# A decoder kernel on one core: first loads in order of use, scores over 32 partitions, conversions behind copies

## The reference

```python
x = LN(x + causal_attention_L0(x))       # 16 heads; q, k of 3 numbers, plus (q.dir)(k.dir); values of 16
x = LN(x + cross_attention_L0(x, ctx))   # 16 heads of 16, scores clipped, nan -> uniform
x = LN(x + sign_ffn_L0(x))               # weights +-1 from booleans: 512(256) -> 1024 -> 1024 -> 256
x = LN(x + grouped_attention_L1(x))      # 16 heads of 64, 4 groups
x = LN(x + cross_attention_L1(x, ctx))   # 8 heads of 64
x = LN(x + experts_L1(x))                # shared expert and top 2 of 8
```

## Time and profile before

| | before |
|---|---|
| runs, us | 1266.02, 1274.17, 1264.87; median 1266.02 |
| the profiled execution | 1272.5 us, its span 1270.6 us |
| PE busy | 1150.3 us, 91% |
| DVE, ACT, POOL busy | 719.7, 565.0, 105.4 us |
| mean granted PE clock | 0.956 |
| chain that ended last | PE 79%, DVE 9%, issue 5%, ACT 4%, DMA 1% |

### The profile page before, as it was taken

One profiled execution on the slowest core, in us unless ns is written; L12 is line 12 of the kernel. 1 busy time (PEld: TensorE's weight loads), 2 busy tenths in 40 slices (PEclk: granted clock), 3 DMA queues, 4 the chain that ended last, 5 costly groups with the idle time before them and its releaser, 6 DMA issues.

```text
span 1270.6 us, 19991 instructions
## 1 busy us (share of the span) xinstructions
PE 1150.3 (91%) x7418; PEld 720.2 (57%) x7418; DVE 719.7 (57%) x1054; ACT 565.0 (44%) x1084; POOL 105.4 (8%) x147
## 2 busy tenths in 40 slices
PE   4999999898988988869988999999999999998797
PEld 2453443442222322247866777877787887786465
DVE  4344445667888789661426466465646666673213
ACT  1344344154545555751214566456635564562210
POOL 0112232112100000010001000010001000100100
PEclk7799899898979999979999999999999999999799
DMA  7012212320000000000023233123634964400000
GB/s 205 14 51 100 89 37 100 115 76 1 1 1 1 1 1 1 1 18 1 1 67 112 62 91 74 34 52 83 150 85 100 214 144 101 101 18 1 1 17 17
DMA packets 56962, 74.20 MB, mean 58 GB/s; under 512 B 12443, under 2 KB 33446, under 8 KB 56870
## 3 DMA queue, kind: packets, MB, share of 16 engines
q1 hardware_dynamic: 53110, 69.26, 21.4%
q10 hardware_dynamic: 3760, 3.67, 0.9%
HBM read 36.20 MB, written 15.73 MB: 41 GB/s over the span
## 4 chain that ended last, share of the span: by engine, by line
PE 79%; DVE 9%; issue 5%; ACT 4%; DMA 1%; POOL 1%; SPq 1%; ACTq 0%; POOLq 0%; DVEq 0%
PE p_unit L1665 20%; PE p_ring L1665 12%; PE p_out L1789 9%; PE p_ring L1685 8%; PE p_ring L1766 8%; PE p_ring L1732 7%; PE p_out L1755 6%; DVE halves L1454 2%; PE p_unit L1857 2%; PE p_ring L1710 1%; ACT prob_b L1238 1%; DVE prob_a L1468 1%; DVE x L1560 1%; PE p_ring L1724 1%; PE p_ring L1703 1%
## 5 line engine op out<-in xcount | busy, mean ns | idle before, releaser
L1454 DVE TENSOR_REDUCE halves<-p_ring 128x2 f32<-128x1024 f32 x128 | 156.2, 1220 | 65.8 <-PE p_ring L1710 65.6
L1252 ACT ACTIVATE prob_a<-p_ring 128x1024 f32<-128x1024 f32 x128 | 130.6, 1022 | 101.6 <-PE p_ring L1732 101.4
L1434 DVE TENSOR_REDUCE nmax<-p_ring 128x2 f32<-128x1024 f32 (+1 forms) x128 | 156.0, 1219 | 33.7 <-PE p_ring L1685 33.6
L1270 ACT ACTIVATE probT_b<-p_ring 128x512 f32<-128x512 f32 x144 | 84.5, 598 | 202.2 <-PE p_ring L1766 200.7
L1238 ACT ACTIVATE prob_b<-p_ring,nmax 128x512 f32<-128x512 f32 (+1 forms) x192 | 158.6, 837 | 18.3 <-DVE nmax L1434 18.0
L1685 PE MATMUL p_ring<-stacks 128*128 128x512 f32 x512 | 151.4, 418 | 8.9 <-ACT prob_b L1238 5.3
L1487 DVE COPY probT_b<-p_ring 128x512 f32<-128x512 f32 x112 | 77.1, 688 | 133.5 <-PE p_ring L1766 133.0
L1766 PE MATMUL p_ring<-ident,prob_b 128*128 128x128 f32 x1024 | 134.5, 274 | 0.3 <-ACT probT_b L1270 0.3
L1766 PEld LDWEIGHTS p_ring<-ident,prob_b 128*128 128x128 f32 x1024 | 116.2, 141 | 23.5 <-issue 14.8
L1732 PE MATMUL p_ring<-x_q,x_kq 32*128 32x512 f32 x512 | 124.4, 658 | 2.9 <-DVE halves L1454 2.9
L1454 DVE TENSOR_REDUCE wide_max<-p_ring 128x2 f32<-128x256 f32 (+3 forms) x64 | 52.6, 823 | 90.3 <-PE p_ring L1703 90.3
(11 more groups left out here) (226 smaller groups left out, 1614.1 us busy)
## 6 DMA issues: line engine op xcount, KB each, us to landing
stacks<-x_kd SPq DMA_DIRECT2D x64, 256.0 KB, 5.9
stacks<-splitH_b SPq DMA_DIRECT2D x80, 128.0 KB, 2.3
stacks<-splitL_b SPq DMA_DIRECT2D x80, 128.0 KB, 2.4
x_kd<-early SPq DMA_DIRECT2D x19, 256.0 KB, 2.0
x_v<-x_vd SPq DMA_DIRECT2D x8, 512.0 KB, 4.1
x_kd<-xT SPq DMA_DIRECT2D x13, 256.0 KB, 2.0
x_vd<-early SPq DMA_DIRECT2D x11, 256.0 KB, 2.0
a_st<-a_image SPq DMA_DIRECT2D x64, 32.0 KB, 1.8
```

Of the source, the lines that this page charges most:

```text
L1252: nc.scalar.activation(prob_place(key), slot_of("S2", key), ACT.Exp, accum_out=x0_sums[:, m:m + 1]).then_inc(done["E2"], 1)
L1270: keep_turned(act, key, lambda o, i: nc.scalar.activation(o, i, ACT.Copy)).then_inc(done["VA"], 1)
L1434: nc.vector.tensor_reduce(nmax[:, n % 4, 0:heads], src, AX.X, ALU.max, negate=True).then_inc(done["M"], 1)
L1454: nc.vector.tensor_reduce(to, src, AX.X, ALU.max, negate=True).then_inc(done["M1"], 1)
```

## The change

1. The first loads. ACT issues only x[0]. SP, after its four small loads, waits for them and for x[0], and then issues `a_wv`, two quarters of the context, the weights of the cross-attention, the other two quarters, x[1], and the rest as before. Each quarter has its semaphore; `a_wv` has its own.
2. The pads `ctx_sum1` and `ctxT1` are cleared by POOL (behind those of `a_v`), with a semaphore of their own, `ctx_ones`, that 65 products wait for besides `ctx_padded`.
3. S1 and S2 of the self-attention read 32 partitions of each head.
4. `FW` 0 and 1 stay behind the last exponential; 2 to 4 stand behind the last `DN`, 5 to 7 behind the first `xT X0 0`; `K2` stands behind the last f0 unit of batch 0; `xT X0 1` comes four ticks after its `LN` (one before).

```diff
-            unit("xT", L, b, 0, after=[later(("LN", (L, b)), 1 if L == "X0" else 2)] if L in ("A0", "X0") else []),
+            unit("xT", L, b, 0, after=[later(("LN", (L, b)), 1 + 3 * b if L == "X0" else 2)] if L in ("A0", "X0") else []),
...
-        [step("FW", o, after=[("E2", last_one)]) for o in range(FF)] + [step("K2"), step("LD", "a1", after=[UD("xT", "X0", 1, 1)])],
+        [step("FW", o, after=[("E2", last_one)] if o < 2 else
+              [("DN", PAIRS[-1])] if o < 5 else [("UP", ("xT", "X0", 0, 1))]) for o in range(FF)]
+        + [step("K2", after=[UD("f0", 0, FF - 1)]), step("LD", "a1", after=[UD("xT", "X0", 1, 1)])],
...
-            sp.dma_start(a0_wv[:, :, :], rows("L0_attn_wv")).then_inc(a0w_loaded, 16)
-
+            sp.wait_ge(a0_loaded, 64)
+            sp.wait_ge(x_loaded[0], 16)
+            sp.dma_start(a0_wv[:, :, :], rows("L0_attn_wv")).then_inc(a0v_loaded, 16)
+
+            def load_context(sg):
+                at = 4 * (sg % 2)
+                sp.dma_start(ctx_raw[:, 4 * sg:4 * sg + 4, :],
+                             d["ctx_768"][sg // 2].rearrange("(i p) c -> p i c", p=128)[:, at:at + 4, :])\
+                  .then_inc(ctx_loaded[sg], 16)
+
+            load_context(0)
+            load_context(1)
...
+            load_context(2)
+            load_context(3)
+            sp.dma_start(x[:, TT:2 * TT, :], d["x"][1].rearrange("(i p) c -> p i c", p=128)).then_inc(x_loaded[1], 16)
...
             blank(a0_v).then_inc(values_cleared, 1)
+            pool.wait_ge(values_cleared, 1)
+            link(nc.gpsimd.memset(ctx_sum1[64:128, :], 512.0))
+            nc.gpsimd.memset(ctxT1[64:128, :], 1.0).then_inc(ctx_ones, 1)
+            pool.wait_ge(ctx_ones, 1)
...
-            for b in range(B):
-                act.dma_start(x[:, b * TT:(b + 1) * TT, :], d["x"][b].rearrange("(i p) c -> p i c", p=128))\
-                   .then_inc(x_loaded[b], 16)
-            act.dma_start(ctx_raw[:, :, :], d["ctx_768"].rearrange("b (i p) c -> p (b i) c", p=128))\
-               .then_inc(ctx_loaded, 16)
+            act.dma_start(x[:, 0:TT, :], d["x"][0].rearrange("(i p) c -> p i c", p=128)).then_inc(x_loaded[0], 16)
...
-            nc.vector.memset(x1_wv1[CC - 128:128, :], 0.0)
-            nc.vector.memset(ctx_sum1[64:128, :], 512.0)
-            nc.vector.memset(ctxT1[64:128, :], 1.0).then_inc(ctx_padded, 1)
+            nc.vector.memset(x1_wv1[CC - 128:128, :], 0.0).then_inc(ctx_padded, 1)
...
-                            nc.tensor.matmul(o[:, aa, 0:w], a0_st[r:r + 17, G % HELD, 1, 128 * i:128 * i + 128],
-                                             a0_st[r:r + 17, G % HELD, 0, 0:w], start=True, stop=False,
+                            nc.tensor.matmul(o[:, aa, 0:w], a0_st[r:r + 32, G % HELD, 1, 128 * i:128 * i + 128],
+                                             a0_st[r:r + 32, G % HELD, 0, 0:w], start=True, stop=False,
...
                         pe.wait_ge(ctx_padded, 1)
+                        pe.wait_ge(ctx_ones, 1)
```

More of the change, by code:

```diff
@@ L773, in decoder @@
         pair_stacked = [sem(f"pair_stacked{s}") for s in range(2)]
-        x_loaded, ctx_loaded = [sem(f"x_loaded{b}") for b in range(B)], sem("ctx_loaded")
-        a0_loaded, a0w_loaded, x0_loaded = sem("a0_loaded"), sem("a0w_loaded"), sem("x0_loaded")
+        x_loaded, ctx_loaded = [sem(f"x_loaded{b}") for b in range(B)], [sem(f"ctx_loaded{j}") for j in range(4)]
+        a0_loaded, a0v_loaded, a0w_loaded, x0_loaded = (sem(n) for n in ("a0_loaded", "a0v_loaded", "a0w_loaded", "x0_loaded"))
         consts_ready = sem("consts_ready")
         pads_cleared, stacks_cleared, values_cleared = sem("pads_cleared"), sem("stacks_cleared"), sem("values_cleared")
-        ctx_padded = sem("ctx_padded")
+        ctx_padded, ctx_ones = sem("ctx_padded"), sem("ctx_ones")
         early_out = [sem(f"early_out{j}") for j in range(EARLY)]
@@ L1724, in _ @@
                                 ins = nc.tensor.matmul(o[:, aa, at:at + T - 128 * c],
-                                                       a0_st[r:r + 17, G % HELD, 0, 128 * c:128 * c + 128],
-                                                       a0_q2[r:r + 17, G % 2, 128 * c:T], start=True, stop=True,
+                                                       a0_st[r:r + 32, G % HELD, 0, 128 * c:128 * c + 128],
+                                                       a0_q2[r:r + 32, G % 2, 128 * c:T], start=True, stop=True,
                                                        tile_position=(r, 0))
@@ L1812, in _ @@
                         _, sg, c = u
-                        pe.wait_ge(ctx_loaded, 16)
+                        pe.wait_ge(ctx_loaded[sg], 16)
                         n = (128, CC - 128)[c]
@@ L1839, in _ @@
                     elif u[0] == "ma":
-                        pe.wait_ge(a0w_loaded, 16 * 3)
+                        pe.wait_ge(a0w_loaded, 16 * 2)
                         wait(pe, "UD", "mv")
@@ L1917, in _ @@
                             elif L == "A0":
-                                pe.wait_ge(a0w_loaded, 16 * 3)
+                                pe.wait_ge(a0v_loaded, 16)
                                 wait_x_turned(pe, "in", b)
```

## The result

| | before | changed |
|---|---|---|
| median (lowest to highest) of 20 runs each, us | 1268.95 (1264.65 to 1274.17) | 1265.39 (1260.11 to 1269.0) |
| ratio, 95% interval | | 0.997 [0.9957, 0.9982] |
| profiled execution, its span, us | 1272.5, 1270.6 | 1264.46, 1262.7 |
| mean granted PE clock | 0.956 | 0.964 |

The changed kernel is 3.6 us faster, where 5.6 was forecast; the time is 1265.4, where 1260 was forecast. The two profiled executions are 8.0 us apart; the one of before lies 3.6 us above its own 20-run median, so the traces say where time moved, and the runs say how much.

A forecast was written before the change was run, and what follows sets the result against it. TensorE, busy 91% of 1270.6 us, was taken as the bound. 1272.5 - 0.5 (start) - 5.1 (end) = 1266.9 for the profiled execution, 1260.4 against the three-run median, stated as 1260; range 1250 to 1267.

The forecast's parts named there:

- 5.0 + 27 x 0.535 = 19.45 [...] From there the chain is as before: Start: SP, after 27 issues, reaches the spreading DMAs at 19.45 instead of 19.89; first score 30.2, gain 0.5 us.
- The lower end: Start: a loss of 1.2 us if x[0] lands at 5.67 and late loads delay the spreading by 1 us more.
- So the cost is nothing, and taken for itself the gain too: Self-attention scores: reading 32 rows instead of 17 neither costs nor gains time by itself.
- Rival B: Self-attention: the 32 rows lift PE's granted clock; 6 us more expected, thus 1254; chance 0.27.
- Half clock for about 19 us between the first score and 60: Sign in PE's clock early in self-attention: about 19 us means clock unchanged, under 12 means rows lift it.
- A: The forecast itself: start and end gains both as computed, 1260 us; chance 0.50.
- The forecast's own alarm: Sign of being wrong: the time between 43 and 540 us changes by over 2 us.
- Rival D: Before the first score: PE's idle 5 us delays the first full-clock stretch, +10.2 us, 1270; chance 0.06.
- The working for the order: End of cross-attention: moving batch 1's turning of x behind six f0 units gives 3.5 of the 5.1 us.
- upper end: End of cross-attention: gain 6.9 us if raw's earlier start lets PE keep its clock over eight output products.
- because POOL's conversion of k2 (1.90 us from 546.05) has moved behind f0: End of cross-attention: batch 0's normalisation then takes 1.38 us instead of 3.05, gaining 1.6 us.
- C: Rival: one half does not pay (start loses 1.2, end gives 2.5, or 65 waits show); 1262 to 1266; chance 0.17.

The follow-up runs named there:

- e3: The kernel before with the new first loads and pads alone (17 rows, old end): 1269.98 us, ratio to before 1.0013.
- e1: The kernel before with one edit, self-attention scores reading 32 partitions instead of 17: 1264.45 us against 1267.88, ratio 0.9980.
- e2: The kernel before with only the new order at the end of the cross-attention: 1265.07 us, ratio to before 0.9973.
- e6: The changed kernel with nine loads not needed early issued behind the first group's stacking DMAs: 1257.26 us, ratio to the kernel before 0.9918.
- e9: The kernel before with only POOL's k2 conversion listed behind f0 of batch 0 and waiting for it: 1263.97 us against 1268.78, ratio 0.9962.
- e5: The changed kernel with POOL's k2 conversion also waiting for DVE's last f0 unit of batch 0: 1260.54 us, against 1267.11 for the kernel before, ratio 0.9948.

## Why the prediction was wrong in its steps

Forecast against runs, in us:

| part | forecast | runs | traces |
|---|---|---|---|
| start: loads and pads | -0.5 | +1.7 (0.4 to 2.9), e3 | first score +2.94 |
| 32 rows | 0 | -2.5 (-1.0 to -3.9), e1 | self-attention 183.9, with 17 rows 184.6, 184.6, 188.1 |
| end | -5.1 | -3.4 (-1.6 to -5.2), e2 | exponential to f1 -2.8 |
| sum | -5.6 | -4.2; the change itself -3.6 | |

The time came out 5.4 us above the 1260: 2.9 because the three runs that it was set against lay low, 2.0 because the gain was smaller, the rest by rounding.

**Start, right.** x[0] in by 5.0: it was 5.21, SP went on at 5.72, and `a_scale` gained nothing for the scores because SP was behind, as forecast. The pads cleared on POOL cost DVE nothing, not even the 2 us that were allowed for.

**Start, failed.** The step "5.0 + 27 x 0.535 = 19.45 [...] From there the chain is as before". Both halves of it were too small. The pitch was taken from issues made in 3.56 to 14.79 us with less queued; in the new order it was 0.565, and with SP's wait until 5.72 that puts the spreading 1.6 us later than forecast. And the landing was copied as 3.51 us although the same paragraph had worked out a backlog lasting until 20.5: the rows show the DMA engines full until 23.1, and 5.43. The lower end allowed 1.2 us of loss, with x[0] at 5.67 and 1 us for the backlog; it left the pitch at 0.535, which was 0.8 us short, and the backlog cost 1.9. e6 shows the cause: without the late loads in front, 18 issues go at 0.483 and the last piece lands after 4.0. The Trainium skill's page "DMA: Bandwidth & Descriptors" (Queues, rings and completion order) says that each DMA engine consumes the descriptors of one issuing sequencer's row in ring order. By that a spreading DMA on SP's row stands behind every load that SP issued, while ACT's loads stood in another row. SP's landing times (5.43 behind its loads, 4.0 in e6, 3.51 before) would agree, but ACT's four spreading DMAs speak against the row as the cause: with no load ahead in their own row (ACT's queue) they took 6.3 to 6.7 us. Engines that are full whatever the row are enough to explain all of them; whether the order within SP's row adds to it stays open.

**Rows, a term of nothing that was 2.5 us.** "So the cost is nothing, and taken for itself the gain too": the cost was nothing, the gain was 2.5 us (1.0 to 3.9) in e1. Rival B had the sign, with 6 us expected; its mechanism, the clock, is possible but not shown. "Half clock for about 19 us between the first score and 60" was to say A and less than 12 B; the changed kernel has 33.6 to 42.4 and 56.1 to 59.9 (part of a stretch until 62.9), 12.6 in all, between the two and close to B's side. Of the 13.6 us less at half clock in the whole self-attention 6.3 lie there and 7.3 behind, where the stretches at 149 and 193 us of the kernel before are gone. The forecast's own alarm, a change of over 2 us between 43 and 540, went off: the first score is 2.94 late and the last exponential 3.7 early. But it was set too fine for one pair of profiles: it goes off between before, e2 and e9 too, which share that code. Rival D did not come: full clock began at 42.4, as before at 42.8. The Trainium skill's "TensorE: Matmul & The Clock Gate" (Part 1) ties the clock to how busy the engine is and names no rows. By that e1 should have changed nothing; e1's time speaks against it, with an interval that ends at 0.9992. The way from rows to time stays open: the mean granted clock over all runs of e1 (0.9641 against 0.9633) shows a part of it at most, since 0.0008 is some 2 us more at full clock, 1 us of time.

**End, right.** The normalisation of batch 0 fell from 3.05 to 1.38 us, and it, not `raw`, released the chain. The working for the order holds too: 3.5 us forecast, 3.2 measured between e9 and e5. The 16 output passes took 3.91 us instead of 4.78, 0.9 us that the forecast had only in its upper end.

**End, failed.** The step "because POOL's conversion of k2 (1.90 us from 546.05) has moved behind f0". It moved behind f0 in the list only. No wait ties POOL to f0, so it ran at 556.50, beside batch 1's normalisation, which took 3.06 us and not the 1.38 that "562.47" was worked out with. That is 1.68 us, on the very path that the reordering had made critical, and f0's last two units, at half clock behind PE's longer idle time, took 1.5 us more. Restored by one wait, the end gives 5.8 us (34.29 - 28.48) against the 5.1 forecast: the sum was about right for a kernel that was not the one at hand. The Trainium skill's "SBUF — State Buffer" (shared port pair) has the loser of that pair fully blocked for the whole instruction. The traces agree as far as one instruction bears the whole loss: the first of the four took 2.10 us instead of 0.41 beside POOL's 1.90. But it had started 0.05 us ahead of POOL's and lost all the same. And not every pair blocks: DVE's clearing of `a_st` kept its 1.34 us beside POOL's clearing of `ctxT`.

**Chances.** The time fell in the range and within 1%, as said. That was luck in part, by errors that cancel: what the start lost, the rows won back. The time, 1265.4, lies in C's range (0.17), not at A's 1260 (0.50); as a gain (3.6 of 5.6) it lies between the two. C's loss at the start, B's rows and a smaller end all happened at once; they had been weighed as if one excluded the others.

## What to carry to other kernels

A step's place in a list orders it only against its own engine's other steps; ask what wait holds it, and what it will run beside when it does start. Loads "in order of use" pay by what is put behind the first small DMAs of the critical path, not by what is put in front: here moving nine unneeded loads away was worth 8.0 us at the first score, and the order that put all loads ahead of the spreading on one issuing engine had cost 2.94. A section of one profiled execution can differ by 6 us from another of the same code; take the size of an effect from many runs, and from a trace only what repeats. When several cheap parts come together, take their costs as a sum with its spread, not as rivals of which one comes true.

## What the runs showed of the hardware

- A matmul over 32 instead of 17 rows takes no longer: the 128 passes of the second scores last 0.215 to 0.791 us in the kernel before and in the changed one. The kernel with 32 rows was 0.2% faster in each of three comparisons, one of them clear of zero.
- DMA issue is not a fixed price: three 0.5 KB loads took 2.71 us of SP's sequencer at a DMA share of 0.99, and 1.38 with less queued.
- The last of four DMAs that spread `a_H` and `a_L` on SP landed 5.43 us after its issue at a share of 1.10, 4.0 at 0.23 and 3.51 at 0.48, so the share when the spreading starts does not order them by itself. ACT's four took 6.3 to 6.7 us among full engines, with no load ahead in their own queue.
- One DVE instruction of 0.41 us took 2.10 beside a POOL conversion of 1.90 us; a DVE clearing beside a POOL clearing was not stretched (1.34 us with and without).
- A wait on one POOL instruction was worth 2.6 to 3.0 us of the path to f1, 1.68 of them DVE's normalisation, the rest mostly PE passes that ran at full instead of half clock.
